# Front and attention in one program, the last fold group among the first attention steps, and feed-forward weights fetched before attention ends

## The reference

```python
h = _layernorm(x) * (1 + ca) + sa
x = x + ga * attention(h)      # 16 heads of 128
h = _layernorm(x) * (1 + cb) + sb
x = x + gb * ffn(h)            # hidden width 1408

# attention: q = rmsnorm(rope(h @ Wq_c @ Wq_up)); one key and value head
# c_out  = softmax over 64 compressed keys (16 tokens each), with a sink
# sw_out = softmax over a window of 128 keys, logits 50*tanh(s/50), with a sink
# result = ((c_out + sw_out) @ Wg per group of 4 heads) @ Wo
# ffn: gate = silu(x @ Wg'), up = x @ Wu', out = (gate * up) @ Wd'
#      each weight is int32: (wq - 128) * scale
```

## Time and profile before

| what | value |
|---|---|
| median of 3 runs | 1029.59 us |
| profiled execution | 1023.58 us |
| its span | 1021.5 us |
| PE busy | 930.4 us (91%) |
| PE weight loads busy | 777.5 us (76%) |
| DVE / ACT / POOL busy | 677.1 / 564.8 / 560.1 us |

### The profile page before, as it was taken

How to read it: one execution, slowest core, us unless ns; L and a number is a source line. 1 busy time by engine, 2 the same in 40 slices (tenths; PEclk the granted TensorE clock), 3 DMA queues, 4 the chain that set the end, 5 groups by cost and what they waited for, 6 DMA issues and landing times. The chain is left out here.

```text
span 1021.5 us, 16023 instructions
## 1 busy us (share of the span) xinstructions
PE 930.4 (91%) x4766; PEld 777.5 (76%) x4766; DVE 677.1 (66%) x1256; ACT 564.8 (55%) x1556; POOL 560.1 (55%) x760
## 2 busy tenths in 40 slices
PE   4989886699999999999999999999668999999996
PEld 4987774577888888887788888888457777878784
DVE  4565495488888888888888888888568442332312
ACT  0554452477777777777777777777231423324221
POOL 0175000588888888888888888887213222222222
PEclk9799898699999999999999999999879999999999
DMA  8757652304024131131221402420180020020101
GB/s 272 225 205 240 255 171 90 114 16 142 17 57 138 46 112 47 57 126 37 88 91 42 142 17 57 139 65 11 43 349 0 1 83 1 1 83 1 42 0 43
DMA packets 52738, 93.66 MB, mean 92 GB/s; under 512 B 9920, under 2 KB 29376, under 8 KB 49728
## 3 DMA queue, kind: packets, MB, share of 16 engines
q1 hardware_dynamic: 42192, 65.30, 20.0%
q10 hardware_dynamic: 10480, 27.47, 7.4%
HBM read 75.33 MB, written 26.08 MB: 99 GB/s over the span
## 5 line engine op out<-in xcount | busy, mean ns | idle before, releaser
L968 PE MATMUL banks<-fold,aoT 128*128 128x512 f32 x768 | 194.2, 402 | 1.4 <-DVE aoT L1149 1.4
L1506 PE MATMUL banks<-hT,w_hi 128*128 128x512 f32 x704 | 172.3, 397 | 14.9 <-DVE w_hi L1555 13.0
L1506 PEld LDWEIGHTS banks<-hT,w_hi 128*128 128x128 f32 x704 | 132.6, 191 | 44.6 <-issue 13.1
L1647 POOL TENSOR_TENSOR gus<-arena,gus 128x512 fp32r<-128x512 f32 x44 | 59.5, 1353 | 194.0 <-ACT gus L1549 194.0
L968 PEld LDWEIGHTS banks<-fold,aoT 128*128 128x128 f32 x768 | 140.7, 190 | 29.5 <-DVE aoT L1149 1.8
L968 PE MATMUL banks<-k_st,qT 128*128 128x320 f32 (+6 forms) x768 | 123.7, 311 | 0.0
L1615 DVE SCALAR_TENSOR_TENSOR arena<-banks,sg,arena 128x512 f32<-128x512 f32 x44 | 33.0, 749 | 122.6 <-ACT arena L1544 122.6
L968 PEld LDWEIGHTS banks<-k_st,qT 128*128 128x128 f32 x768 | 110.0, 192 | 0.2
L1544 ACT ACTIVATE arena<-banks,sg 128x512 f32<-128x512 f32 x44 | 30.3, 689 | 136.4 <-PE banks L1506 136.4
L1473 PE MATMUL banks<-w_hi,gus 128*128 128x512 f32 x352 | 90.8, 398 | 10.8 <-POOL gus L1647 8.7
L968 PE MATMUL banks<-pp,v_st 128*128 128x512 f32 x360 | 99.5, 410 | 0.0
(11 more groups left out here) (185 smaller groups left out, 1971.2 us busy)
## 6 DMA issues: line engine op xcount, KB each, us to landing
arena<-in_wq_blocks ACTq DMA_DIRECT2D x8, 1056.0 KB, 4.9
wq_words<-in_wq_blocks ACTq DMA_DIRECT2D x8, 1056.0 KB, 7.0
w_lo<-wq_words SPq DMA_DIRECT2D x11, 768.0 KB, 14.2
go_raw<-in_w_go SPq DMA_DIRECT2D x16, 512.0 KB, 5.7
arena<-in_L_attn_h SPq DMA_DIRECT2D x16, 256.0 KB, 5.6
comp_raw<-in_w_comp SPq DMA_DIRECT2D x16, 256.0 KB, 5.3
v_parts<-v_out ACTq DMA_DIRECT2D x4, 1024.0 KB, 4.5
k_st<-k_parts SPq DMA_DIRECT2D x32, 128.0 KB, 2.5
```

The costliest lines, as they stand in the source:

```text
L968: last = pe.matmul(out, lhs[a], rhs[b], start=start and q == 0 and u == 0, stop=stop and q == n - 1 and u == 2)
L1506: last = pe.matmul(GU[2 * (n % 2) + w][:], parts[a][:, h, cols], hT[:, c % 2, x, k], start=(k == 0 and q == 0), stop=(k == KC - 1 and q == ...
L1647: pool.tensor_tensor(gus[:, n % 2, 1], gu[:, n % 2], gus[:, n % 2, 0].bitcast(F32), ALU.subtract).then_inc(gu_lo, 1)
```

## The change

The front's and the attention's programs become plain functions, called one after the other for each engine within one block: there is no barrier between them, and attention's buffers lie where they don't disturb what still runs. In detail:

- The last fold group (pieces 12 to 15) leaves the front. It becomes four **units**, one for each head: `unit(pe, f)` does the twelve matmuls of head f over all four pieces, `unit_high` and `unit_low` take them out. Unit 0 stands ahead of query(0), unit 1 behind it, unit 2 behind query(1), unit 3 behind query(3). PSUM banks change sides: attention's Q, T, O, Y are banks 4 to 7, the scores 0 to 3.
- SP issues the loads of tiles 0 and 1 behind `load_go(11)`, then the last four pieces, then x of tiles 0 and 1.
- Two weight blocks are fetched in attention, behind `load_x(15)`, into memory that the queries' weights have left, and `first_weights` on DVE makes their high parts behind the last `tile_out`, ahead of the flag.
- In feed-forward ACT makes the high parts of the other nine blocks (`weight_parts`), one per block behind its own high part of gate x up.
- POOL computes the deviation behind its low part of block 3 (chunk 0) or 4 instead of ahead of it; DVE's statistics and z move with it and in chunk 0 are cut in halves.
- DVE gates all four tiles at once (`gate_tiles`) and adds two behind each of the next two blocks (`add_tiles`).
- The very last low part is DVE's, and the last `down` reports tile by tile.

```diff
+UNIT_BANK = (0, 1, 6, 7)
+UNIT_FREE = (5, 6, 11, 12)
...
-        for n in range(10, STEPS):
-            load_go(n)
...
+        for n in range(10, STEPS - HG):
+            load_go(sp, n)
...
-            elif n == 14:
-                dve.wait_ge(sd_in, 16)
+            elif n == 11:
+                dve.wait_ge(late_in, 32)
                 for b in range(BATCH):
...
-        for n in range(3, STEPS):
+        for n in range(3, STEPS - HG):
             fold_step(n)
+
+    def unit(pe, f):
+
+        g = GPT - 1
+        pe.wait_ge(f_lo, UNIT_FREE[f])
+        for i in range(HG):
+            pe.wait_ge(go_lo, HG * g + i + 1)
+            for u, (a, b) in enumerate(((0, 0), (0, 1), (1, 0))):
+                last = pe.matmul(bank[UNIT_BANK[f]][:], go[:, i, a, f * P:(f + 1) * P], go[:, i, b, C:2 * C],
+                                 start=(i == 0 and u == 0), stop=(i == HG - 1 and u == 2))
+        last.then_inc(unit_mm, 1)
...
         def query(g):
+            if opening(g, 0):
+                units.unit(pe, 0)
+                pe.wait_ge(units.up_lo, 1)
+                pe.wait_ge(units.f_lo, 2 * HG + 1)
...
+            for c, f in ((0, 1), (1, 2), (3, 3)):
+                if opening(g, c):
+                    units.unit(pe, f)
...
+        units.stored(sp)
+        for t in range(2):
+            load(t, t)
+        units.load_rest(sp)
+        sp.wait_ge(units.sd_done, 1)
+        for t in range(2):
+            load_x(t, t)
...
             if t == TILES - 3:
                 load_x(TILES - 1, (TILES - 1) % 2)
+                sp.wait_ge(words_out, 16 * PIECES)
+                sp.wait_ge(s["q_mm"], GROUPS)
+                for h in range(AHEAD_WEIGHTS):
+                    load_weights(sp, h, w_lo, wq_words, w_in)
...
+        def first_weights():
+            wait(dve, "wp_mm", GROUPS - GPT + 1)
+            for h in range(AHEAD_WEIGHTS):
+                weight_high(dve, h, w_hi, w_lo, w_in).then_inc(hi_early, 1)
...
-              alone=EVERY, after={2: first_statistics, 3: first_normal})
+              alone=EVERY, after={2: first_statistics, 3: first_normal, 4: first_weights})
...
+        def weight_parts(h):
+            act.wait_ge(w_in[h], 16)
+            act.activation(w_hi[:, PLACE[h]], w_lo[:, PLACE[h]].bitcast(I32), ACT.Identity, bias=minus_zero[:, 0:1]
+                           ).then_inc(hi_done, 1)
...
+                if n == HB * CHUNKS - 1:
+                    dve.wait_ge(gu_hi, n + 1)
+                    dve.tensor_tensor(gus[:, n % 2, 1], gu[:, n % 2], gus[:, n % 2, 0].bitcast(F32),
+                                      ALU.subtract).then_inc(gu_last, 1)
+                if c == 0 and h + 1 < HB:
+                    weight_low(h + 1)
+                if c and h == 0:
+                    gate_tiles(c - 1)
+                if c and h in (0, 1):
+                    add_tiles(c - 1, ready[h])
```

More of the change, by code:

```diff
@@ L138, in build_program @@
[L138 to L144 removed]
+                buffers = attention_buffers(sb, scope)
@@ new lines, in build_program @@
+                sem = semaphores(nc, scope)
+                front, units = front_programs(
+                    sem, banks, bank, own, x_tok, W_qkv, W_comp, W_go, Wq_up, q_w, k_w, sink, cond, wmod, s_down, table, kons,
+                    ident, csil, arena, q_parts, k_parts, v_parts, ck_parts, ckq_parts, sinkb, sink_e, fold, ga, wup, modT2,
+                    row, norm["z"], go_raw, go, raw_up)
+                attention = attention_programs(
+                    sem, buffers, units, banks, bank, x_tok, x_mid, q_parts, k_parts, v_parts, ck_parts, ckq_parts, table,
+                    kons, ident, low, wup, fold, sinkb, sink_e, ga, wq_blocks, wq_words, words_out, s_blocks, sg, arena,
+                    inexact, xs_ffn, xs_in, norm, w_hi, w_lo, w_in, hi_early)
@@ new lines, in _ @@
+                def _(pool):
+                    front.gpsimd(pool)
+                    attention.gpsimd(pool)
+                @block.tensor
+                def _(pe):
+                    front.tensor(pe)
+                    attention.tensor(pe)
+        with ExitStack() as scope:
+            sb(scope, "weights", [P, 2, HB, WB], F32R)
+            ffn_block(nc, scope, sb, bank, x_mid, out_tok, ident, arena, xs_ffn, xs_in, wq_words, sg, row,
+                      modT2, inexact, norm, w_hi, w_lo, w_in, hi_early)
@@ L147, in semaphores @@
+Programs = namedtuple("Programs", "sync scalar vector gpsimd tensor")
+Units = namedtuple("Units", "load_rest stored late_in rope_in sink_steps up_lo go_lo f_lo sd_done unit high low")
 def semaphores(nc, scope, prefix=""):
@@ new lines, in attention_programs @@
+def attention_programs(sem, buffers, units, banks, bank, x_tok, x_mid, q_parts, k_parts, v_parts, ck_parts, ckq_parts, table, kons,
+                       ident, low, wup, fold, sinkb, sink_e, ga, wq_blocks, wq_words, words_out, s_blocks, sg, arena, inexact,
+                       xs_ffn, xs_in, norm, w_hi, w_lo, w_in, hi_early):
+    MASKED, WHOLE = 0, 1
+    (logits, cs, prob, ws, wr, cmx, csm, crs, squares_w, flag, ones, pp, pcS, aoT, y_t, x_t, pc, q_st, rope_st, k_st,
+     v_st, ck_st, sq, ss, rq, exponent, epsilon, qn, ropb, qT) = (buffers[n] for n in (
+         "logits cs prob ws wr cmx csm crs squares_w flag ones pp pcS aoT y_t x_t pc q_st rope_st k_st v_st ck_st sq "
+         "ss rq exponent epsilon qn ropb2 qT").split())
+    minus_zero = norm["minus_zero"]
@@ L1081, in probs_high @@
         def probs_high(g):
+            if opening(g, 0):
+                units.high(act, 3)
             wait(act, "pT_mm", g.n())
@@ L1094, in squares @@
         def squares(g):
+            if opening(g, 0):
+                units.high(act, 0)
             wait(act, "q_mm", g.n())
@@ L1099, in squares @@
             last.then_inc(s["q_sq"], 1)
+            if opening(g, 0):
+                units.high(act, 1)
         def query_high(g):
@@ L1104, in query_high @@
             act.activation(qT[:, g.slot, 0], T[:], ACT.Copy).then_inc(s["qT_hi"], 1)
+            if opening(g, 0):
+                units.high(act, 2)
         def compressed_exp(g):
@@ L1171, in probs_low @@
         def probs_low(g):
+            if opening(g, 0):
+                units.low(dve, 3)
             wait(dve, "p_hi", g.n())
@@ L1198, in scale_query @@
                               rq[:, g.slot].unsqueeze(2).broadcast_to([P, HG, D]), ALU.mult).then_inc(s["q_sc"], 1)
+            if opening(g, 0):
+                units.low(dve, 1)
         def compressed_sum(g):
```

397 lines of the change are left out of this document (210 added, 187 removed).

## The result

| | before | after |
|---|---|---|
| median (runs) | 1029.54 us (4) | 1002.18 us (4) |
| lowest to highest | 1025.08 to 1030.93 | 999.27 to 1007.18 |
| profiled execution / span | 1023.58 / 1021.5 us | 999.27 / 997.5 us |

A forecast was written before the change was run, and what follows sets the result against it. PE fills 49.45 of 50 us in mid-attention, so gains lie where PE waits. Six terms sum to 26.5 us: 1023.58 to 997.1, plus 6.0 to the median, 1003 us; range 995 to 1012.

The forecast's parts named there:

- The opening: Start of attention: query(0) 12.4 us earlier, second scores at 185 instead of 196.19; 11 us gained, bounds 6 and 14.5.
- rival A: Opening: SP's loads delay the pieces or units fall on the chain, giving 5 us instead of 11; 1009, chance 0.12.
- The sign of a wrong forecast: Opening: a wait of 3 us of `transpose_probs` behind unit 3 would show the forecast wrong.
- The hand-over: Attention to feed-forward: prefetched weights save 4.2 us, POOL held beside DVE's parts costs 1.9; 2.3 us gained (1.5 to 4.5).
- Chunk 0: Feed-forward, chunk 0: deviation behind POOL's low part removes most of 6.0 us, 2 come back; 4.0 us gained (0 to 6).
- rival B: Feed-forward's chunk 0 stays as it is; chunk 0 and deviation terms give 1.5 us in all; 1009, chance 0.10.
- Boundaries: Feed-forward's chunk boundaries: gates on DVE no longer wait for adds; 3.75 us gained (3 to 3.75).
- The deviation in chunks 1 and 2: Feed-forward, chunks 1 and 2: deviation behind POOL's low part has 4 us of room; 3.4 us gained (1.5 to 3.4).
- The end: Kernel's end: last low part on DVE, gates wait only for the first `down` tile; 2.0 us gained (1.5 to 2.2).
- Rival C: Opening: PE's granted clock stays at 1.00, 4 us more there and 4.2 at the hand-over; 997, chance 0.09.
- Rivals D and E: D: longer period in attention, 1037, chance 0.03; E: query(0) waits for something at the old time, 1014, chance 0.04.

The follow-up runs named there:

- e1: The changed kernel run again with no edit: 999.24 us, ratio 0.9727 to the kernel before.
- e11: The changed kernel without edit, run beside the two variants with several edits: 1002.03 us, ratio 0.9754 to the kernel before.
- e4: Changed kernel with ACT's weight high parts made in the first six blocks of chunk 0: 1001.2 us, ratio 0.9721 to the kernel before.
- e6: Changed kernel without prefetch, both early weight blocks loaded by feed-forward: 1001.82 us, ratio 0.9743 to the kernel before.
- e7: Changed kernel with POOL's deviation ahead of the low part again, in block 3 of chunks 0 to 2: 1006.81 us, ratio 0.9794 to the kernel before.
- e8: Changed kernel with DVE's gate and add alternating per tile again at chunk boundaries: 1004.19 us, ratio 0.9741 to the kernel before.
- e2: Changed kernel with SP issuing the last fold pieces ahead of the loads of tiles 0 and 1: 999.2 us, ratio 0.9701 to the kernel before.
- e9: Changed kernel with last pieces loaded first, unit 3 behind query(2) and weight parts in the first six blocks: 988.47 us, ratio 0.963 to the kernel before.
- e3: Changed kernel with unit 3 behind query(2) instead of behind query(3): 994.0 us, ratio 0.9649 to the kernel before.
- e5: Changed kernel with all four units ahead of query(0), still without the barrier: 1006.45 us, ratio 0.9794 to the kernel before.
- e12: The kernel before, unedited, profiled a second time: 1031.37 us, span 1029.4 us.
- e10: Changed kernel with unit 3 behind query(2) and weight parts in the first six blocks: 992.7 us, ratio 0.9673 to the kernel before.

## Why the prediction was right, point by point

**The time.** 1003 against 1002.18 us. The sum of terms was 26.5 us and the profiles differ by 24.0, but those two numbers compare badly: the front's length by chance took 5.1, and parts that I had put at nothing gave some. Taken from E on, the changed kernel gained 29.1 us in the first profile, 27.8 in e1 and 27.0 in e11; the medians differ by 27.4, 28.5 and 24.2. So the size was right, but terms that were too large and too small by 1 to 3 us cancel in it, and that the median was met to 1 us is partly luck.

**1. The opening, 11 us.** Right in mechanism and in size: 12.3 in the first profile. That one was lucky. The seven profiles with the changed opening (the first, e1, e4, e6, e7, e8, e11) have the second scores 27.7 to 33.6 us behind E, the middle one 30.4: 9.7 gained, and all within the bounds of 6 and 14.5. The steps inside it were missed both ways. Piece 15 was put at 159, 2.8 us behind E; that held in the first profile (2.7), but in the others it is used 3.7 to 6.0 us behind E, as it takes 7.5 to 9.1 us to land. So query(0), put 12.4 us earlier, came 12.6 earlier in the first profile and 10.9 in the middle one. Here the argument against rival A, that the DMA engines are nearly idle, did not carry over: they are busy now, and piece 15 takes 3.7 and 3.9 us to land in e2 and e9, where it goes ahead of the tiles' loads. Query(0) to query(3), put at 18 to 19.5 us, took 16.6 to 17.3; the granted clock from query(0) to the second scores was 0.80 to 0.92, before 0.58. Unit 3, put at 1.5 to 3 us given back, cost more: from query(3) to the second scores it is 5.2 us in the first profile and 6.0 to 6.7 in the others, against 2.1 before, so 3.1 to 4.5. The sign of a wrong forecast, a wait of 3 us of `transpose_probs` behind unit 3, did come: it starts 4.86 us behind the start of query(3), where it was 1.42. Placed behind query(2) the unit costs nothing (e3): query(0) to query(3) stays at 16.6 us, and the second scores follow by 1.1. By e5 some 3 us of the gain are the barrier's and 6.5 the interleaving's. Rival A's 5 us are out, though its cause has a share of 2 us.

**2. The hand-over, 2.3.** 3.0 against the first profile of the kernel before and 2.2 against e12, with the prefetch's part shown by e6. The mis-sized step was POOL's: held for 0.64 us, not the 1.9 I chose from bounds of 0 and 2.6. I took the length of all of DVE's work. In fact POOL waited only for the part that ran when it came, and the second part waited for POOL. From ACT's first channel part on 4.3 us were gained, as said; ahead of it another 0.6 us were lost, which e6 loses too, without the weight parts, and which stay open. The Trainium skill (GPSIMD Engine Reference, Key points) says that the two contend for SBUF, and the rows agree: POOL's add takes 0.64 us more beside the weight parts. They also show who pays: one instruction runs at its usual length and the other waits. The low part of 3.84 us in the earlier trace rows is the other extreme: there the rest of one DVE instruction and two whole ones went ahead of POOL's. Why POOL got in between two DVE instructions at the hand-over and not there is open.

**3. Chunk 0, 4.0.** Only 1.4, the one term that was clearly wrong; rival B left next to nothing for it. The failed step is ACT's: "In blocks 7 to 9 it runs into the moment at which ACT must empty a bank between the two halves of PE's step: 0.5 us each." The place was right, the size not: 1.2 us each, 3.6 in all, since ACT's whole part (1.5 us) and then both channel reads stand ahead of PE's second half, and PE starts that half slower (2.11 us for eight matmuls against 1.81). Without it e4 comes to the 4.0 and more. The reading of the 6.0 us was off as well. The steps of chunk 0 before show 4.7 us in the one step that waits for the deviation (10.12 against 5.44), of which e7 brings back 3.7, and 1.2 in the step of 7.16, where POOL's low part of 3.84 us stands. That second loss is not the deviation's, and in the changed kernel ACT's part takes its place: 7.12. The first two steps take 10.1 us instead of 9.4, as the first `down` waits for a low part of POOL that has no slack yet. POOL's low part beside `weight_low` takes 2.08 us instead of 1.29 and hid in its slack, as said.

**4. Boundaries, 3.75.** Before 12.14 for two steps, after 10.88: 1.26 each, 3.8 us. By e8 the gates' order alone is 2.8 of it, and 1.0 is each gate's wait for the add before it; the cause named was both.

**5. The deviation in chunks 1 and 2, 3.4.** Steps of 7.14 and 7.13 became 5.44: 3.4 us; e7 brings back 1.82 and 2.00.

**6. The end, 2.0.** From the start of the last gate-and-up to the first gate 9.35 us before, 7.36 after. But behind it 1.2 us were lost again, which I had put at nothing: SP's four stores take 4.00 us to issue from 990.60. The other profiles of this end show 0.7 to 1.0 us lost (e10 1.45), and 0.5 less than that against e12. Why the issue is longer was not tried.

**Not predicted.** The last tile of attention took 26.0 us instead of 27.7, with the fold's matmuls of the drain at 2.98 us instead of 4.59: a stretch at the other clock level. Over the twelve profiles of the changed kernel and its kin it is 26.0 us in eight and 27.7 in four, in both of the kernel before 27.7; kernels that differ only in feed-forward or in the opening show both values. So chance has a part in it, and whether the change has one is open. Rival C's idea, a better clock, held in the opening (0.94 against 0.74 from E to the second scores); it was no term of its own, and e3's run at 1.00 shows what was left. Rivals D and E are out: attention's middle is 49.48 of 50 us busy.

## What to carry to other kernels

Work that waits for nothing belongs into gaps where the engine waits on a latency chain, at a place where the next thing on the chain isn't due: moving one 2.8 us unit from behind query(3) to behind query(2) was worth 4 to 5 us. A load that moves ahead of urgent ones costs them more than its issue: here the last of them took 6.5 us and more to land instead of 3.4. When helper work is spread evenly over blocks, ask in which blocks the engine has a deadline within its step, and put the work in the others. And where a front varies by 8 us between runs of the same program, compare stretches that begin at the same event, since neither the spans nor medians of six runs tell 3 us.

## What the hardware showed that I had not expected

- POOL and DVE hold each other one at a time, and in the rows that I compared the one that comes first is not slowed. POOL came 0.16 us after a DVE part of 0.95 us: its add took 1.91 us instead of 1.27, the DVE part behind it 2.02 instead of 0.95. POOL's subtraction takes 2.08 instead of 1.29 when it comes behind the start of `weight_low`, which keeps its 1.75. In the kernel before, where POOL came 0.04 us ahead of it, POOL kept its 1.29 and `weight_low` took 2.87:

```profile
758.20 1.29 POOL L1647 TENSOR_TENSOR gus<-arena,gus 128x512 fp32r<-128x512 f32 x1 [24.37 <-ACT gus L1549]
758.24 2.87 DVE L1559 SCALAR_TENSOR_TENSOR w_lo<-w_lo,w_hi 128x1536 fp32r<-128x1536 int32 x1
```

- The same front took 155.6 to 164.4 us. The first visible difference is a group of 32 narrow matmuls at about 24 us: 3.76 to 3.98 us in the first profile of the kernel before and in four of the changed one and its kin, 6.83 in the first of the changed kernel and as slow in the rest, at a granted clock of 0.90 to 1.00 in the quick groups and 1.00 in the slow ones. In the five profiles with the quick group the clock falls behind it (0.73 to 0.80 over 20 to 45 us, 1.00 in the others), and still their fronts are the shorter ones: E at 155.6 to 158.6, in the others at 157.8 to 164.4. What decides it is open.
- A short wait can cost as much again behind it: in e7 PE waited 1.85 us after dense work at a granted clock of 1.00, the clock in the `down` behind it was 0.56 and then 0.50, and this `down` took 1.8 us longer.
